# Masked relative queries: from GpSimd, 32 queries at a time into one buffer, to ScalarE, column by column into one of two

## The chip, the cores and the metric

One core of a Trainium2 chip runs the whole program in one launch. The metric is the device time in microseconds (us), a median over runs. Engines are named as in the profile: PE is TensorE (PEld its weight loads), DVE is VectorE, ACT is ScalarE, POOL is GpSimd, SP is SyncE, which here only issues DMAs.

## The reference

A transformer layer over x of shape (16, 1024, 256), with 16 heads of 16:

```python
h = layernorm(x)
q, k, v = heads(h @ Wq.T + bq), heads(h @ Wk.T + bk), heads(h @ Wv.T + bv)
rel = rel_emb[r[None, :] - r[:, None] + 511]        # (1024, 1024, 16)
qk = einsum('bhld,bhrd->bhlr', q, k) / 4 + einsum('bhld,lrd->bhlr', q, rel)
x = x + layernorm(softmax(qk) @ v  -> heads joined @ Wo.T + bo)
x = x + layernorm(base + shared low-rank + routed low-rank, top 2 of 6 experts)
```

Indices of `rel_emb` outside its 1023 rows are clamped. What matters here is the second term of `qk`: for every query its own window of the relative embeddings.

## The kernel before

**Tiles and groups.** The 16 x 1024 rows are 128 tiles (`NT`) of 128 queries. A tile's attention is 16 groups (`NG`), g = 4 jp + k: jp picks 256 of the batch's 1024 keys, k picks 32 of the tile's 128 queries, for all heads. One group's scores are 128 keys x (16 heads x 32 queries), twice (c = 0, 1), in two of PSUM's six score banks; three such pairs (`NBUF`) go round.

**A group on the engines.** PE writes the scores in `scores`: 8 matmuls of `ks` by `qm` (L724) and 12 of the shifted embeddings `tw` by the masked queries `rm` (L730) for each c. DVE takes maxima (L1185), PE transposes them (L738), DVE reduces and spreads them (`spread`: L1194, then `nmm`, L1197), PE adds the negative maxima to the scores (`shift`, L747), and ACT makes `prob` by one Exp (`exp`, L1018). PE multiplies by the values (`pv`, L757) in the next stage's groups k = 1 and 2. PE is one group ahead: its group g ends with the shift of group g - 1, and ACT's group g ends (`before`) with the Exp of group g - 1. So the Exp of a tile's group 14 follows the shift that is PE's last work of the tile, and that of group 15 comes in the next tile's group 0.

**Work of other tiles between.** `wide` and `mixed` on PE, `side` on DVE, the copies in ACT's `tile` and POOL's `tile` carry the projections of the tile 8 later, the output side of the tile before, and the feed-forward part of the one before that. Every engine works through an order written out by hand, and waits on semaphores.

**The masked queries.** `raw` holds the tile's queries in 24 copies of 16 rows (8 groups of 16 partitions x 3 column sets s), which SP loads with 24 DMAs (`load_raw`). `rm` is `raw` times `mask_r`, which is 1 where a partition belongs to a column and 0 elsewhere: for every octet of queries, ten column slots (3 + 4 + 3, `RUNS`). Before the change POOL's `mask(i)` writes the part for the 32 queries i by three multiplications (L592), in one buffer. Part i is last read by group 12 + i, so POOL waits for that group's scores:

```python
if att:                                   # early in the tile
    pool.wait_ge(s_scores, t * NG)
    mask(NI - 1)                          # part 3 of this tile
...
pool.wait_ge(s_raw, ...)                  # late in the tile
pool.wait_ge(s_scores, t * NG + NG - NI + 1)
mask(0)                                   # part 0 of the next tile; then rs2, parts 1 and 2, res
```

PE waits for part k in groups 0 to 3 (L884). SP waits for part 3 before it loads the next tile's queries into `qm` and `raw` (L411). Before the loop POOL writes parts 0 to 2 of the first tile, between the seventh and the eighth split of the prologue's queries and keys.

**The loop.** Tiles 2 to 127 run in a loop of three turns of 42 tiles; `ph` is the tile's number modulo the buffers.

Of the kernel before, what the change touches and what calls it, by code (L numbers as in the profile page):

```python
# [9 lines left out]
H, HD = 16, 16  # L10
# [3 lines left out]
P = 128  # L14
NT = B * L // P
TPB = L // P
JC = L // P
NJP = JC // 2
IW = 32
NI = P // IW  # L20
NG = NJP * NI
# [4 lines left out]
OCT = 8  # L26
RP = 3
RUNS = ((0, 3), (2, 4), (5, 3))
# [16 lines left out]
def sandwich_kernel(nc, x, wqT, bq, wkT, bk, wvT, bv, woT, bo, relT, baseT, base_b,  # L45
# [13 lines left out]
    with ctx:  # L59
        def sb(name, shape, dt=f32):  # L60
            return ctx.enter_context(nc.sbuf_tensor(name, shape, dt))
# [6 lines left out]
        ident16 = sb("ident16", [P, P], f16)  # L68
        pick = sb("pick", [P, H // 2, P], f16)
        mask_h = sb("mask_h", [H, 2, IW], f16)  # L70
        mask_r = sb("mask_r", [P, RN], f16)
        mhalf = sb("mhalf", [P, 1])
        eps = sb("eps", [P, 1])
        one = sb("one", [P, 1])
# [27 lines left out]
        vs = sb("vs", [P, JC, H, 32])  # L102
        raw = sb("raw", [P, RP, H, P], f16)
        qm = sb("qm", [ROWS, 2, H, P], f16)
        rm = sb("rm", [P, NI, IW // OCT, RN * H], f16)
        prob = sb("prob", [P, 2, 2, H, P])
        r1 = sb("r1", [P, H + P], f16)
        nm = sb("nm", [P, 2, P], f16)
# [219 lines left out]
        def _(sp):  # L328
# [63 lines left out]
            def after(sem, value):  # L392


                sp.wait_ge(sem, value)
                sp.sem_inc(s_step, 1)

            def tile(b, it, att, proj, a, bb, new=False, last=False, end=False, wrap=False, first=False):
# [4 lines left out]
                if att:  # L403
                    if not first:

                        after(s_scores, t * NG)
                        load_window(it, NJP - 1)
                        if new:
                            after(s_qkst, n * 64)
                            load_keys(b, NJP - 1)  # L410
                    after(s_mask, t * NI + NI)  # L411
                    if last:
                        load_queries(b + 1, 0)
                        load_raw(b + 1, 0)
                    else:
                        load_queries(b, it + 1)
                        load_raw(b, it + 1)
# [116 lines left out]
        def _(pool):  # L534
# [50 lines left out]
                keep(mask_r[:, c:c + n], ALU.is_ge, lo + half - 1, [[half, n]], -1)  # L585
            pool.drain().then_inc(s_cpool, 1)

            def mask(i):

                for s, ((q, n), c) in enumerate(zip(RUNS, RCOL)):  # L590
                    src = raw[:, s, :, i * IW:(i + 1) * IW].rearrange("p h (m e) -> p m h e", e=OCT)
                    last = g.tensor_tensor(rm[:, i, :, c * H:(c + n) * H].rearrange("p m (h e) -> p m h e", e=n),  # L592
                                           src[:, :, :, q:q + n],
                                           mask_r[:, c:c + n].rearrange("p (a b e) -> p a b e", a=1, b=1)
                                           .to_broadcast((P, IW // OCT, H, n)), ALU.mult)
                last.then_inc(s_mask, 1)

            def rstd(dst, mv, ve):
                g.tensor_tensor(ve[:, :], mv[:, 1:2], eps[:, :], ALU.add)  # L599
                pool.drain()  # L600
# [12 lines left out]
                return x.rearrange("p c i -> p (c i)")  # L613

            def tile(t, n, att, proj, a, b, ph=None):
                if att:
                    pool.wait_ge(s_scores, t * NG)
                    mask(NI - 1)
                if b:
                    pool.wait_ge(s_x1T, t - 1)  # L620
                    split([flat(x1T2[:, k, :, :]) for k in range(2)], flat(x1T[:, :, :]), s_x1T2)
# [54 lines left out]
                if a:  # L676
                    pool.wait_ge(s_xr, t * 16)
                    pool.wait_ge(s_yn, t)
                    g.tensor_tensor(x1[:, :], yn[:, :], xr[:, :], ALU.add).then_inc(s_x1, 1)
                if att:  # L680

                    pool.wait_ge(s_raw, t * (RP * OCT * 16) + 2 * RP * OCT * 16)
                    pool.wait_ge(s_scores, t * NG + NG - NI + 1)
                    mask(0)
                if a:
                    pool.wait_ge(s_mv2, t)
                    rstd(rs2, mv2, ve2).then_inc(s_rs2, 1)
                if att:
                    for i in range(1, NI - 1):
                        pool.wait_ge(s_scores, t * NG + NG - NI + i + 1)  # L690
                        mask(i)
                if b:
                    pool.wait_ge(s_y2n, t - 1)
                    pool.wait_ge(s_out, (t - 1) * 16)
# [4 lines left out]
            pool.wait_ge(s_mv0, 1)  # L699
            rstd(rs0, mv0, ve0).then_inc(s_rs0, 1)  # L700
            for k in range(TPB):
                if k == TPB - 1:
                    pool.wait_ge(s_raw, RP * OCT * 16)
                    for i in range(NI - 1):
                        mask(i)
                pool.wait_ge(s_qkbp, k + 1)
                if k > 1:
                    pool.wait_ge(s_qkst, (k - 1) * 64)
                split([flat(first_h[k % 2][:, :, :]), flat(first_l[k % 2][:, :, :])], flat(qkb[:, :, :]), s_qksp)
# [4 lines left out]
        def _(pe):  # L714
            mm = nc.tensor.matmul

            def scores(g, c, buf, qb):

                jp, i = divmod(g, NI)
                bank = sc[:, 2 * buf + c, :]  # L720
                out3 = bank.rearrange("p (h i) -> p h i", i=IW)
                j = (2 * jp + c) * P
                for h in range(H // 2):
                    last = mm(bank[:, 2 * h * IW:(2 * h + 2) * IW], ks[:, h, j:j + P],  # L724
                              qm[:, qb, 2 * h:2 * h + 2, i * IW:(i + 1) * IW],
                              start=(h == 0), stop=False, skip_group_check=True)
                for m in range(IW // OCT):
                    u = P - 1 - (i * IW + OCT * m) + c * P
                    for s, ((q, n), r) in enumerate(zip(RUNS, RCOL)):
                        last = mm(out3[:, :, OCT * m + q:OCT * m + q + n], tw[:, s, jp, u:u + P],  # L730
                                  rm[:, i, m, r * H:(r + n) * H].rearrange("p (h e) -> p h e", e=n),
                                  start=False, stop=False, skip_group_check=True)
                return last

# [137 lines left out]
            def tile(t, n, att, proj, a, b, ph=None):  # L872
                read = None
                for g in range(NG):
                    jp, k = divmod(g, NI)
                    old = a if g == 0 else att
                    if att:
                        if k == 0:
                            pe.wait_ge(s_tw[jp], t * 16 + 16)
                            pe.wait_ge(s_ks[jp], batch_of(t) * 96 + 96)  # L880
                        if g == 0:
                            pe.wait_ge(s_qm, t * 96 + 96)
                        if jp == 0:
                            pe.wait_ge(s_mask, t * NI + k + 1)  # L884
                        free = t * NG + g - NBUF + 1
                        if not (isinstance(free, int) and free <= 0):
                            pe.wait_ge(s_exp, free)
                        scores(g, 0, buffer(ph, g), ph % 2)
                    if read is not None:
                        pe.wait_ge(*read)  # L890
                    if old:
                        transpose_max(t * NG + g)
                    if att:
                        scores(g, 1, buffer(ph, g), ph % 2).then_inc(s_scores, 1)

                    wide(t, n, g, att, proj, a)
                    read = mixed(t, g, att, a, b)
                    if old:
                        shift(buffer(ph, g - 1), t * NG + g)
# [43 lines left out]
        def _(act):  # L943
# [56 lines left out]
            for k in range(TPB):  # L1000
# [8 lines left out]
                if k == 4:  # L1009
                    first_keys()  # L1010

            def exp(g, buf, count, free):

                jp, i = divmod(g, NI)
# [12 lines left out]
            def tile(t, n, att, proj, a, b, ph=None):  # L1027
                for g in range(NG):
# [54 lines left out]
                        copy(oT[:, :, :].rearrange("p c i -> p (c i)"), p_t).then_inc(s_oT, 1)  # L1083
                    if a if g == 0 else att:
                        before(g, t, ph)

            passes(act, tile)


# [235 lines left out]
```

## Time and profile before

| | |
|---|---|
| median of 3 runs | 5952.92 us (5951.9 to 5957.06) |
| the profiled execution's own time | 5973.55 us |
| its span in the trace | 5971.8 us |
| PE busy | 5815.1 us, 97% |
| DVE, POOL, ACT busy | 4903.6, 3328.2, 3069.3 us (82%, 56%, 51%) |
| POOL's multiplications for `rm` | 1545, 929.9 us |
| granted TensorE clock, mean | 0.994 |

The profiled execution is 0.35% longer than the median; times of single instructions come from it. A span of 5971.8 us over 128 tiles, with some 73 us ahead of the first scores and 50 us behind the last, is about 45.7 us for a tile and 2.86 us for a group.

### The profile page before, as it was taken

The page shows a single profiled execution, that of the slowest core. Times are in us where ns is not written, and L with a number is a line of the kernel's source. Part 1 is how long each engine was busy: PE and PEld are TensorE (multiplying, and loading weights), DVE is VectorE, ACT ScalarE, POOL GpSimd, SP SyncE. Part 2 cuts the span into 40 slices and gives each one's busy share as a digit, 9 for nine tenths or more (in the row PEclk, how much of TensorE's full clock was granted, in tenths as well). Part 3 has the DMA queues.
Part 4 walks back from the last instruction along what each step waited for, and adds up shares of the span by engine and source line. Part 5 has one row for each costly group of instructions (what it writes and reads, how often), then busy time and mean ns, then how long its engine had stood idle before and what let it go on. Part 6 is the DMA issues. An engine that isn't in the chain of part 4 may idle for free.

```text
span 5971.8 us, 378300 instructions
## 1 busy us (share of the span) xinstructions
PE 5815.1 (97%) x161792; PEld 5385.6 (90%) x161792; DVE 4903.6 (82%) x10178; ACT 3069.3 (51%) x5160; POOL 3328.2 (56%) x5182
## 2 busy tenths in 40 slices
PE   6999999999999999999999999999999999999997
PEld 5999999999999999999999899999999999999996
DVE  5888888888888888888888888888888888888886
ACT  3555555555555555555555555555555555555554
POOL 4555555555555555555555555555555555555555
PEclk8999999999999999999999999999999999999998
DMA  5343343443434334343343434334344343433432
GB/s 152 85 102 94 91 116 85 106 102 86 113 91 115 88 87 114 93 110 90 92 110 90 112 94 100 95 90 117 83 107 100 89 110 90 116 87 88 113 95 53
DMA packets 1461087, 589.65 MB, mean 99 GB/s; under 512 B 1127168, under 2 KB 1425136, under 8 KB 1459376
## 3 DMA queue, kind: packets, MB, share of 16 engines
q1 hardware_dynamic: 1454752, 562.48, 37.8%
q8 instruction: 1288, 21.10, 1.6%
q14 instruction: 423, 3.47, 0.2%
q10 hardware_dynamic: 4624, 2.60, 0.2%
HBM read 476.43 MB, written 89.85 MB: 95 GB/s over the span
## 4 chain that ended last, share of the span: by engine, by line
PE 83%; DVE 10%; issue 3%; DVEq 2%; POOL 1%; SPq 0%; POOLq 0%; DMA 0%; ACT 0%
PE sc L730 21%; PE pw L757 15%; PE sc L747 15%; PE sc L724 14%; DVE r L1185 5%; PE pm L778 4%; PE pw L778 4%; PE pm L738 4%; PE pw L764 3%; DVE xn L1099 2%; DVE nmm L1197 1%; DVEq L1196 1%; DVE y2n L1099 1%; PE pm L797 1%; DVEq L1095 1%
## 5 line engine op out<-in xcount | busy, mean ns | idle before, releaser
L1185 DVE TRANSPOSE_TENSOR_REDUCE r<-sc 128x32 f16<-128x1024 f32 x2048 | 2542.9, 1242 | 22.3 <-PE sc L730 19.0
L1018 ACT ACTIVATE prob<-sc 128x1024 f32<-128x1024 f32 x2048 | 2098.8, 1025 | 213.9 <-PE sc L747 176.9
L730 PE MATMUL sc<-rm,tw 128*128 128x48 f16 (+1 forms) x49152 | 2144.6, 194 | 11.6 <-issue 11.4
L730 PEld LDWEIGHTS sc<-rm,tw 128*128 128x128 f16 x49152 | 1754.4, 100 | 13.6 <-issue 13.2
L724 PE MATMUL sc<-qm,ks 96*128 96x64 f16 x32768 | 1635.8, 193 | 23.2 <-POOL rm L592 13.8
L747 PE MATMUL sc<-nmm,pick 128*128 128x64 f16 x32768 | 1297.5, 193 | 40.5 <-DVE nmm L1197 32.1
L724 PEld LDWEIGHTS sc<-qm,ks 96*128 96x128 f16 x32768 | 1298.3, 98 | 35.2 <-issue 21.9
L1194 DVE TENSOR_REDUCE nm<-pm 16x32 f16<-16x256 f32 x2048 | 834.8, 408 | 557.5 <-PE pm L738 540.9
L747 PEld LDWEIGHTS sc<-nmm,pick 128*128 128x128 f16 x32768 | 1128.7, 98 | 179.2 <-DVE nmm L1197 91.3
L757 PE MATMUL pw<-prob,vs 128*32 128x128 f32 x32768 | 1117.9, 276 | 12.5 <-issue 8.1
L757 PEld LDWEIGHTS pw<-prob,vs 128*32 128x32 f32 x32768 | 840.1, 109 | 76.0 <-issue 14.6
L592 POOL TENSOR_TENSOR rm<-raw,mask_r 128x192 f16<-128x192 f16 (+1 forms) x1545 | 888.8, 605 | 20.8 <-DMA raw<-qk_s 18.2
L1197 DVE TENSOR_TENSOR nmm<-nm,mask_h 16x64 f16<-16x64 f16 x2048 | 652.3, 319 | 194.0 <-issue 5.4
L738 PE MATMUL pm<-ident,r 128*128 128x128 f16 x4096 | 571.0, 221 | 1.3 <-issue 0.7
L947 ACT ACTIVATE ot<-pw 128x512 f32<-128x512 f32 x512 | 305.2, 596 | 488.4 <-PE pw L757 488.4
L605 POOL TENSOR_TENSOR oT<-oT,one 128x256 f16<-128x256 f32 x128 | 78.6, 614 | 759.8 <-ACT oT L947 759.8
L947 ACT ACTIVATE nmt<-pm 128x16 f32<-128x16 f32 x512 | 94.3, 184 | 760.0 <-PE pm L797 760.0
L634 POOL TENSOR_TENSOR wp<-parts,wst 128x1088 f32<-128x1088 f32 x128 | 262.7, 2053 | 178.9 <-ACT parts L947 178.9
L764 PE MATMUL pw<-ident,ot 128*128 128x128 f32 x2048 | 324.9, 281 | 0.8 <-ACT ot L947 0.7
L601 POOL TENSOR_TENSOR rs<-ve,mhalf 128x1 f32<-128x1 f32 x513 | 282.2, 550 | 73.7 <-issue 1.3
L605 POOL TENSOR_TENSOR hT<-hT,one 112x128 f16<-112x128 f32 x128 | 51.2, 400 | 488.1 <-ACT hT L947 488.1
L599 POOL TENSOR_TENSOR ve<-mv,eps 128x1 f32<-128x1 f32 x513 | 113.6, 221 | 373.8 <-DVE mv L1096 373.5
(153 smaller groups left out, 5766.2 us busy)
## 6 DMA issues: line engine op xcount, KB each, us to landing
raw<-qk_s SPq DMA_DIRECT2D x3096, 64.0 KB, 2.9
tw<-tw_s SPq DMA_DIRECT2D x512, 288.0 KB, 4.0
v_s<-vpad SPq DMA_DIRECT2D x136, 256.0 KB, 3.4
vs<-v_s SPq DMA_DIRECT2D x64, 512.0 KB, 4.4
qm<-qk_s SPq DMA_DIRECT2D x768, 32.0 KB, 2.1
ks<-qk_s SPq DMA_DIRECT2D x378, 64.0 KB, 3.4
qk_s<-qkh SPq DMA_DIRECT2D x272, 64.0 KB, 2.9
qk_s<-qkl SPq DMA_DIRECT2D x272, 64.0 KB, 2.6
```

What stands on the lines that cost most here:

```text
L592: last = g.tensor_tensor(rm[:, i, :, c * H:(c + n) * H].rearrange("p m (h e) -> p m h e", e=n), src[:, :, :, q:q + n], mask_r[:, c:c + n]. ...
L724: last = mm(bank[:, 2 * h * IW:(2 * h + 2) * IW], ks[:, h, j:j + P], qm[:, qb, 2 * h:2 * h + 2, i * IW:(i + 1) * IW], start=(h == 0), stop ...
L730: last = mm(out3[:, :, OCT * m + q:OCT * m + q + n], tw[:, s, jp, u:u + P], rm[:, i, m, r * H:(r + n) * H].rearrange("p (h e) -> p h e", e=n),
L738: last = mm(p_max[:, c * P:(c + 1) * P], r1[:, c * H:c * H + P], ident16[:, :], start=True, stop=True)
L747: last = mm(pairs[:, :, h, :], pick[:, h, :], nmm[:, :, :], start=False, stop=True, skip_group_check=True)
L757: last = mm(pw[32 * q:32 * q + 32, col * P:(col + 1) * P], vs[:, 2 * jp + c, h, :], prob[:, jp % 2, c, h, :], start=(c == 0), stop=(c == 1))
L764: last = nc.tensor.transpose(pw[:, col * P:(col + 1) * P], ot[:, col, :], ident[:, :])
L778: last = mm(dst, lhs, rhs, start=(m == 0), stop=(m == len(steps) - 1))
L1018: A(prob[:, jp % 2, :, :, i * IW:(i + 1) * IW], sc[:, 2 * buf:2 * buf + 2, :].rearrange("p c (h i) -> p c h i", i=IW), ACT.Exp).then_inc(s ...
L1185: v.tensor_reduce(r1[:, 0:2 * H], sc[:, 2 * buf:2 * buf + 2, :].rearrange("p c (h i) -> p (c h) i", i=IW), axis=AX.X, op=ALU.max, apply_tr ...
L1194: v.tensor_reduce(part, p_max[0:H, :].rearrange("h (q i) -> h i q", i=IW), axis=AX.X, op=ALU.max, negate=True).then_inc(s_nmr, 1)
L1197: v.tensor_tensor(nmm[0:H, :, :], part.rearrange("h (a i) -> h a i", a=1) .to_broadcast((H, 2, IW)), mask_h[:, :, :], ALU.mult).then_inc(s ...
```

## The change

Ten ScalarE operations a tile take the place of POOL's twelve multiplications. Each scales one column slot of `raw` (128 partitions x 256 elements) by one float32 column of `mask_r` (L71, now f32) and writes it to its place in `rm`, which has two halves, one for even and one for odd tiles (L105). In a tile's groups 11 to 15 ACT writes two slots each for the next tile, behind the Exp of `before`; the signal follows the last slot. PE waits for it once a tile, ahead of group 0, in the place of the four waits; SP's wait asks for it by the new count. All slots of tile 0 are written by ACT ahead of its loop. The diff, cut to its core:

```diff
-        mask_r = sb("mask_r", [P, RN], f16)
+        mask_r = sb("mask_r", [P, RN])
-        rm = sb("rm", [P, NI, IW // OCT, RN * H], f16)
+        rm = sb("rm", [P, 2, NI, IW // OCT, RN * H], f16)
@@ SP, tile @@
-                    after(s_mask, t * NI + NI)
+                    after(s_mask, t + 1)
@@ POOL: mask(i) and its calls are gone, in tile and ahead of it @@
-                if att:
-                    pool.wait_ge(s_scores, t * NG)
-                    mask(NI - 1)
...
-                    pool.wait_ge(s_raw, t * (RP * OCT * 16) + 2 * RP * OCT * 16)
-                    pool.wait_ge(s_scores, t * NG + NG - NI + 1)
-                    mask(0)
...
-                    for i in range(1, NI - 1):
-                        pool.wait_ge(s_scores, t * NG + NG - NI + i + 1)
-                        mask(i)
@@ PE, scores and tile @@
-                                  rm[:, i, m, r * H:(r + n) * H]...
+                                  rm[:, qb, i, m, r * H:(r + n) * H]...
                         if g == 0:
                             pe.wait_ge(s_qm, t * 96 + 96)
-                        if jp == 0:
-                            pe.wait_ge(s_mask, t * NI + k + 1)
+                            pe.wait_ge(s_mask, t + 1)
@@ ACT @@
+            def mask(qb, some):
+                for s, q, c, n, e in some:
+                    dst = rm[:, qb, :, :, c * H:(c + n) * H].rearrange("p i m (h e) -> p (i m) h e", e=n)[:, :, :, e]
+                    src = raw[:, s, :, :].rearrange("p h (m e) -> p m h e", e=OCT)[:, :, :, q]
+                    last = A(dst, src, ACT.Identity, scale=mask_r[:, c + e:c + e + 1])
+                return last
...
                     if a if g == 0 else att:
                         before(g, t, ph)
+                    if att and g > 10:
+                        if g == 11:
+                            act.wait_ge(s_raw, t * (RP * OCT * 16) + 2 * RP * OCT * 16)
+                        last = mask((ph + 1) % 2, slots[2 * (g - 11):2 * (g - 10)])
+                        if g == NG - 1:
+                            last.then_inc(s_mask, 1)
+
+            act.wait_ge(s_raw, RP * OCT * 16)
+            mask(0, slots).then_inc(s_mask, 1)
             passes(act, tile)
```

## Rows read from the trace of the kernel before

**Rows 1.** The page: busy time by engine, and the chain that ended last.

```profile
PE 5815.1 (97%) x161792; PEld 5385.6 (90%) x161792; DVE 4903.6 (82%) x10178; ACT 3069.3 (51%) x5160; POOL 3328.2 (56%) x5182
...
PE 83%; DVE 10%; issue 3%; DVEq 2%; POOL 1%; SPq 0%; POOLq 0%; DMA 0%; ACT 0%
```

**Rows 2.** Waits of PE: waited for, us in total, times, longest us.

```profile
PE sc L747 <- DVE nmm L1197: 32.1, 133, 2.2
...
PE sc L724 <- POOL rm L592: 13.8, 3, 10.8
```

**Rows 3.** Timeline, turn of a tile: start us, us, engine, line, work, [idle before].

```profile
3042.85 3.46 POOL L592 TENSOR_TENSOR rm<-raw,mask_r 128x192 f16<-128x192 f16 x6
...
3043.16 0.63 PE L747 MATMUL sc<-nmm,pick 128*128 128x64 f16 x16
...
3043.63 0.40 PE L724 MATMUL sc<-qm,ks 96*128 96x64 f16 x8
3043.83 1.02 ACT L1018 ACTIVATE prob<-sc 128x1024 f32<-128x1024 f32 x1
...
3044.34 0.40 PE L724 MATMUL sc<-qm,ks 96*128 96x64 f16 x8
...
3045.14 0.56 DVE L1197 TENSOR_TENSOR nmm<-nm,mask_h 16x64 f16<-16x64 f16 x1
3045.18 0.38 PE L769 MATMUL pm<-ident,xn 128*128 128x128 f32 x2
...
3045.76 0.64 PE L747 MATMUL sc<-nmm,pick 128*128 128x64 f16 x16 [0.19 <-DVE nmm L1197]
```

**Rows 4.** Timeline of ACT, an Exp with other work queued behind it.

```profile
3049.52 1.03 ACT L1018 ACTIVATE prob<-sc 128x1024 f32<-128x1024 f32 x1 [0.38 <-PE sc L747]
3050.44 0.25 ACT L1056 ACTIVATE wst<-dm 128x64 f32<-128x64 f32 x1
```

**Rows 5.** Groups of instructions by form: busy us, mean ns; idle before, releaser.

```profile
L947 ACT ACTIVATE hT<-pm 112x128 f32<-112x128 f32 x128 | 35.5, 278 | 206.7 <-PE pm L824 206.7
...
L1005 ACT ACTIVATE qkb<-sc,b_qk 128x128 f32<-128x128 f32 x32 | 9.1, 368 | 36.1 <-PE sc L778 25.9 <-POOL qkl L607 10.3
L947 ACT ACT_TABLE_LOAD x1 | 1.3, 1283 | 9.2 <-issue 9.2
...
L947 ACT ACTIVATE w_b<-w_b 112x256 f16<-112x256 f32 x1 | 0.4, 398 | 0.0
```

**Rows 6.** The same view, POOL.

```profile
L592 POOL TENSOR_TENSOR rm<-raw,mask_r 128x256 f16<-128x256 f16 x515 | 314.7, 611 | 0.0
```

**Rows 7.** Line L1197: durations in ns min/median/max, first and last start.

```profile
L1197 DVE TENSOR_TENSOR nmm<-nm,mask_h x2048: 178/180/1056, 75.8 to 5923.9; 16x64 f16<-16x64 f16 x187
```

**Rows 8.** Busy PE in four stretches: PE busy (instructions), granted clock, DMA share, GB/s.

```profile
79.48:82.89 3.41, 1.59 (x49) 1.00 0.57 161
82.89:86.30 3.41, 1.03 (x16) 0.50 0.99 246
5554.46:5561.30 6.84, 5.14 (x144) 1.00 0.80 196
5926.51:5933.33 6.82, 4.40 (x75) 0.75 0.14 41
```

**Rows 9.** Timeline of the prologue's end and of tile 0's group 4.

```profile
69.33 5.07 POOL L592 TENSOR_TENSOR rm<-raw,mask_r 128x192 f16<-128x192 f16 x9 [9.37 <-DMA raw<-qk_s]
71.18 0.59 PE L724 MATMUL sc<-qm,ks 96*128 96x64 f16 x8 [10.84 <-POOL rm L592]
...
87.53 0.58 PE L724 MATMUL sc<-qm,ks 96*128 96x64 f16 x8 [3.25 <-issue]
...
88.77 0.63 PE L724 MATMUL sc<-qm,ks 96*128 96x64 f16 x8
```

**Rows 10.** Waits of SP's queue.

```profile
SPq L479 <- POOL qkl L607: 10.0, 2, 9.8
```

More of the change, by code:

```diff
@@ L586, in _ @@
             pool.drain().then_inc(s_cpool, 1)
[L588 to L596, printed above, removed]
             def rstd(dst, mv, ve):
@@ L679, in tile @@
                     g.tensor_tensor(x1[:, :], yn[:, :], xr[:, :], ALU.add).then_inc(s_x1, 1)
-                if att:
-                    pool.wait_ge(s_raw, t * (RP * OCT * 16) + 2 * RP * OCT * 16)
-                    pool.wait_ge(s_scores, t * NG + NG - NI + 1)
-                    mask(0)
                 if a:
@@ L687, in tile @@
                     rstd(rs2, mv2, ve2).then_inc(s_rs2, 1)
-                if att:
-                    for i in range(1, NI - 1):
-                        pool.wait_ge(s_scores, t * NG + NG - NI + i + 1)
-                        mask(i)
                 if b:
@@ L701, in _ @@
             for k in range(TPB):
[L702 to L705, printed above, removed]
                 pool.wait_ge(s_qkbp, k + 1)
@@ L730, in scores @@
                         last = mm(out3[:, :, OCT * m + q:OCT * m + q + n], tw[:, s, jp, u:u + P],
-                                  rm[:, i, m, r * H:(r + n) * H].rearrange("p (h e) -> p h e", e=n),
+                                  rm[:, qb, i, m, r * H:(r + n) * H].rearrange("p (h e) -> p h e", e=n),
                                   start=False, stop=False, skip_group_check=True)
@@ L1010, in _ @@
                     first_keys()
+            slots = [(s, q + e, c, n, e) for s, ((q, n), c) in enumerate(zip(RUNS, RCOL)) for e in range(n)]
+            def mask(qb, some):
[4 more added lines that the diff above has]
+                return last
             def exp(g, buf, count, free):
```

## The prediction

> **What bounds the kernel now.** I began with the page [rows 1]: PE is busy for 97% of the span and carries 83% of the chain that ended last; DVE has 10% of it, ACT none. So time is won only where PE waits, and lost wherever PE is made to wait. The second view was PE's waits [rows 2]. The largest steady one is the shift waiting for `nmm`, 32.1 us in 133 waits, that is about once a tile and 0.2 us each. PE's wait for POOL's `rm` is 13.8 us, of which 10.8 us is the single wait ahead of the first tile; in the loop POOL's masks are nearly free for PE. The third view was the timeline at the turn of a tile [rows 3], where the reader is to see the order of three things. PE's last shift of the tile, that of group 14, starts at 3043.16. The next tile's first scores start at 3043.63, with no wait. The Exp of group 14 starts only at 3043.83, because it needs that shift. So at the turn ACT is behind PE, and all that stands behind that Exp in ACT's order comes later still.
>
> **What is removed.** POOL loses twelve multiplications a tile. They cost PE almost nothing directly. Indirectly they reach PE through DVE: `nmm` takes 0.56 us at 3045.14 while POOL is masking and 0.18 us otherwise [rows 3, 7], and this is the once-a-tile wait. If `nmm` takes 0.18 us, the shift is held by the transposes ahead of it (3045.18, 0.38 us) instead. The gain is at least the 0.19 us that PE is shown idle, and at most what `nmm` shrinks by, 0.38 us. I take 0.3 us a tile: the transposes' duration overlaps what follows, so the shift can start somewhat before their end.
>
> **What is added on ACT.** Ten Identity operations a tile of 256 elements, SBUF to f16 in SBUF, with a per-partition scale. No row has this. A copy of 256 elements SBUF to f16 takes 398 ns; a column operand adds 368 - 278 = 90 ns (two forms with 128 elements, with and without a bias column) [rows 5]. Together 0.49 us. The bounds: 0.40 us, if the column costs nothing here; above, the strided read and write may cost, for which the nearest row is POOL's multiplication with the same pattern and as many elements, 0.61 us [rows 6], and with the column 0.70 us. I take 0.49 us, since ACT's rows otherwise follow the count of elements. Work queued behind an Exp starts 0.92 us after the Exp's start, 0.11 us before its end [rows 4]; so a second mask starts 0.38 us after the first. Over the tile that is ten times 0.38, 3.8 us more for an engine busy 51%. In groups 11 to 14 it lies under PE's work: a pair adds 0.76 us after an Exp, so ACT is free 1.7 us after the Exp began, in a group of 2.86 us, and the next thing in ACT's order, a copy of what PE makes in the middle or at the end of the group, comes later than that or just then. Without this cover a pair would cost 0.76 us a group.
>
> The masks bring Identity between Exps. The trace shows one table load, at the start, although Identity (`qkb`) ran after Copy and before Exp [rows 5]; so I cost switches at nothing. The Trainium skill, "ScalarE: Activation LUTs", section "What ACT_TABLE_LOAD costs", puts 2.66 us on every switch to another set; by it, were Identity in another set, five groups would pay two switches each, 27 us a tile. The row speaks for one set.
>
> **What is moved: the wait at the turn.** The last pair of masks stands behind the Exp of group 14, and PE may not start the next tile's group 0 before its signal. From [rows 3]: Exp starts 3043.83; first mask 3044.75; second 3045.13; its end 3045.62; the signal and PE's start some 0.05 us later, 3045.67, as PE's start at 3045.76 follows the end of `nmm` at 3045.70 by 0.06. PE would have started at 3043.63. The wait costs 2.04 us. Nothing stands against it: behind the waiting instruction on PE are all of group 0's scores, on which DVE's next maxima and ACT's next Exp depend, so all three stop. What DVE gets is that it has finished group 15's maxima meanwhile; this is why I count the 0.3 us above as given back in full and no more. With the bounds of the mask: 0.20 (3043.63 to the Exp) + 0.92 + 0.29 (0.40 less the overlap of 0.11) + 0.40 + 0.05 = 1.86 us with the cheap one, and 0.20 + 0.92 + 0.59 + 0.70 + 0.05 = 2.46 us with the dear one. Net for a tile 2.04 - 0.3 = 1.74 us; at the bounds 1.86 - 0.38 = 1.48 and 2.46 - 0.19 = 2.27 us. It is paid at the start of tiles 1 to 127: 127 x 1.74 = 221 us (188 to 288).
>
> **The clock.** A PE that pauses can lose its clock. The stretch 79.48 to 82.89, which ends in an idle of about 1.8 us, is followed by one at a granted clock of 0.50, the lower level of 1.2 GHz; the stretch from 5554.46, with 1.7 us of idle in all, stays at 1.00, 2.4 GHz [rows 8]. The new pause would show as 3045.67 - 3043.79 = 1.9 us of idle, right between. Price: 5926.51 to 5933.33 has a mean of 0.75, half of it slow, so a slow stretch can be 3.4 us. At the slow clock the first half of a group took 88.77 - 87.53 = 1.24 us [rows 9], at the full one 3044.34 - 3043.63 = 0.71 us [rows 3]; 3.4 us slow do the work of 1.95 to 2.1 us, so about 1.3 us is lost. I let this happen in a third of the tiles: 42 x 1.3 = 55 us; in none it is 0, in all 165 us.
>
> [...]
>
> **SP and the start.** SP's count changes, and the signal comes 3045.62 instead of the end of part 3's masks, so the loads of `qm` and `raw` move by a few us, with a whole tile to land. They are hidden; without this cover PE would wait at group 0 for `qm`, and ACT at group 11 for `raw`. At the start ACT's ten masks follow the landing of `raw` at 69.33: 9 x 0.38 + 0.49 = 3.9 us, so PE starts at 73.3, not 71.18 [rows 9]: +2.1 us. But POOL's last split of the prologue no longer waits behind nine multiplications; SP's wait of 9.8 us for it [rows 10] goes, the first batch's keys land before group 4, and its wait of 3.25 us and the similar 2.2 us ahead of a shift [rows 2, 9] go, with the slow clock that follows them (about 10 us at 0.50, some 3.9 us). Sum: -7 us.
>
> **The sum.** Against the profiled execution, 5973.55 us: +221 + 55 - 7 = +269 us. That execution is 0.35% above the median of the runs; the same added to the median gives 5952.9 + 269 = 6222 us.
>
> **The rivals.**
> The pause at the turn without any loss of the clock: for it speaks the stretch at 5554.46. 5953 + 221 - 7 = 6167 us.
> The pause and a slow stretch in every tile: for it speaks 79.48, and that the pause comes at the same place each time; against it that 1.9 us is at the edge. 5953 + 221 + 165 - 7 = 6332 us.
> A mask far above 0.70 us because of 2-byte elements at a stride: each 0.1 us more is 127 x 0.2 = 25 us, and from about 1 us a pair would also press on groups 11 to 14: 6400 us and more. No row of ACT has such a pattern.
> No difference: the pause eats waits that PE has anyway. Against it: all of PE's waits in the loop together are far below 221 us [rows 1, 2].
> Faster: ACT is done with the last masks when PE comes to group 0, that is 2.04 us earlier than I work out, before its Exp has even begun. Then the relief of DVE by POOL is all that is left: 5953 - 38 - 7 = 5908 us. The point that decides is the order Exp, masks, signal at the turn; [rows 3] speak against it plainly.
>
> **How the numbers follow.** The pause with some slow stretches 0.50; without any 0.25; with one every tile 0.15; masks far dearer 0.05; no difference 0.03; faster 0.02. The predicted time is that of the first, 6222 us. Its own range with the bounds of the mask is 6160 to 6300. The range for 8 in 10 reaches down past the case without a slow clock and its lower bound, 5953 + 188 - 7 = 6134, and up to the case with one in every tile: 6120 to 6335. Slower by over 0.2% (about what a measurement of this kernel can tell from no change) 0.95, within 0.03, faster 0.02.
>
> **What would show it.** PE's wait at L724 for ACT's `rm`, 127 times with about 1.9 us each, 240 us in all; in the timeline of a turn, Exp, two masks, then PE's first scores. 1290 masks of 0.49 us in ACT's groups, ACT busy about 630 us more, POOL 930 us less. The 32.1 us of waits for `nmm` reduced to a few. A mean granted clock of about 0.98; 0.99 would mean the second case, 0.96 the third. Wrong I would be if that wait were absent or under 1 us, if masks took 0.7 us or more, or if PE waited in groups 11 to 15.

## The result and the profile after

The changed kernel takes 6371.9 us (median of 4 runs, 6367.24 to 6385.57) against 5954.99 us before: a ratio of 1.0704, 95% interval 1.0685 to 1.0722. It is slower, as forecast, but by 417 us and not by 269; 6372 lies above the range of 6120 to 6335 us. The profiled execution took 6385.57 us with a span of 6383.8 us, 412 us more than before.

The page of the changed kernel: busy time by engine, its chain by engine and by line (L698, L704, L721 and L731 are L724, L730, L747 and L757 of before), and its masks:

```profile
PE 5936.7 (93%) x161792; PEld 5568.1 (87%) x161792; DVE 4716.7 (74%) x10178; ACT 3873.6 (61%) x6450; POOL 2470.7 (39%) x3637
...
PE 87%; ACT 9%; issue 2%; DVE 1%; DVEq 1%; SPq 0%; POOL 0%; POOLq 0%; ACTq 0%; DMA 0%
PE sc L704 22%; PE pw L731 16%; PE sc L721 15%; PE sc L698 15%; ACT rm L992 4%; PE pm L752 4%; PE pm L712 4%; PE pw L752 4%; ACT prob L1001 4%; PE pw L738 3%; PE pm L743 1%; PE pm L771 1%; PE pw L743 1%; ACT parts L920 1%; PE pm L798 1%
...
L992 ACT ACTIVATE rm<-raw,mask_r 128x256 f16<-128x256 f16 x1290 | 925.1, 799 | 6.2 <-DMA raw<-qk_s 6.2
```

ACT had 0% of the chain [rows 1]; now it has 9% of it, 4% each in the masks and the Exp. DVE's 10% has shrunk to 1%. A mask takes 799 ns on average. The trace still holds a single table load of 1283 ns, so Identity between the Exps costs no switch. ACT is busy 804 us more than before where 630 were forecast, POOL 857 us less where 930 were. Two of PE's waits in the changed kernel (us in total, times, longest):

```profile
PE sc L698 <- ACT rm L992: 352.5, 128, 13.6
...
PE sc L721 <- DVE nmm L1188: 4.3, 15, 1.1
```

The wait for the masks, less the first tile's 13.6 us, is 338.9 / 127 = 2.67 us of idle a turn. The wait for `nmm`, 32.1 us [rows 2], is nearly gone. One turn in the changed kernel's timeline (start us, us, work):

```profile
2999.26 0.63 PE L721 MATMUL sc<-nmm,pick 128*128 128x64 f16 x16
...
2999.90 0.39 ACT L920 ACTIVATE parts<-pw 128x272 f32<-128x272 f32 x1
3000.17 1.02 ACT L1001 ACTIVATE prob<-sc 128x1024 f32<-128x1024 f32 x1
3000.18 0.37 DVE L1090 TENSOR_SCALAR xn<-x,mv,rs 128x256 f32<-128x256 f32 x1
...
3001.08 1.37 ACT L992 ACTIVATE rm<-raw,mask_r 128x256 f16<-128x256 f16 x2
3002.57 0.60 PE L698 MATMUL sc<-qm,ks 96*128 96x64 f16 x8 [2.68 <-ACT rm L992]
...
3005.80 1.06 PE L721 MATMUL sc<-nmm,pick 128*128 128x64 f16 x16
```

The order is as forecast: PE's last shift, the Exp, two masks, PE's first scores. In [rows 3] the scores follow the start of that shift by 0.47 us, here by 3.31 us: the pause is 2.84 us from start to start, where 2.04 was forecast. Then the shift of 16 matmuls takes 1.06 us instead of 0.64. The same stretch in windows of PE (PE busy, instructions, granted clock, DMA share, GB/s):

```profile
2999.60:3002.57 2.97, 0.29 (x10) 0.90 0.45 140
3002.57:3005.80 3.23, 3.23 (x47) 0.50 0.23 54
3005.80:3009.02 3.22, 3.22 (x60) 0.53 0.36 79
```

After the pause PE works at the lower level of its clock. The mean granted clock is 0.960, where 0.994 was before.

For what follows I measured the turn on the starts of the shifts (L747 before, L721 after): from the shift of group 14 to that of group 15, and from there to that of group 0, as medians over tiles 2 to 127. Before: 2.96 and 3.02 us. After: 6.20 and 3.33 us.

### The profile page after: what moved, and what is told of

Read it like the earlier page. It is cut to its first block, busy times and chain, and to the rows that moved or that the text cites. A ratio compares the mean times of both kernels' runs of the same rounds, so it can differ in the third digit from the quotient of the medians.

```text
span 6383.8 us, 377318 instructions
## 1 busy us (share of the span) xinstructions
PE 5936.7 (93%) x161792; PEld 5568.1 (87%) x161792; DVE 4716.7 (74%) x10178; ACT 3873.6 (61%) x6450; POOL 2470.7 (39%) x3637
## 4 chain that ended last, share of the span: by engine, by line
PE 87%; ACT 9%; issue 2%; DVE 1%; DVEq 1%; SPq 0%; POOL 0%; POOLq 0%; ACTq 0%; DMA 0%
PE sc L704 22%; PE pw L731 16%; PE sc L721 15%; PE sc L698 15%; ACT rm L992 4%; PE pm L752 4%; PE pm L712 4%; PE pw L752 4%; ACT prob L1001 4%; PE pw L738 3%; PE pm L743 1%; PE pm L771 1%; PE pw L743 1%; ACT parts L920 1%; PE pm L798 1%
## 5 line engine op out<-in xcount | busy, mean ns | idle before, releaser
L704 PE MATMUL sc<-rm,tw 128*128 128x48 f16 (+1 forms) x49152 | 2209.1, 197 | 6.3 <-issue 6.1
L698 PE MATMUL sc<-qm,ks 96*128 96x64 f16 x32768 | 1686.1, 195 | 354.2 <-ACT rm L992 352.5
L704 PEld LDWEIGHTS sc<-rm,tw 128*128 128x128 f16 x49152 | 1816.7, 102 | 7.0 <-issue 6.9
L698 PEld LDWEIGHTS sc<-qm,ks 96*128 96x128 f16 x32768 | 1347.8, 100 | 369.2 <-issue 369.2
L721 PE MATMUL sc<-nmm,pick 128*128 128x64 f16 x32768 | 1326.1, 195 | 11.3 <-issue 5.6
L721 PEld LDWEIGHTS sc<-nmm,pick 128*128 128x128 f16 x32768 | 1179.7, 99 | 118.4 <-issue 58.3
L731 PE MATMUL pw<-prob,vs 128*32 128x128 f32 x32768 | 1112.4, 276 | 9.2 <-issue 4.6
L992 ACT ACTIVATE rm<-raw,mask_r 128x256 f16<-128x256 f16 x1290 | 925.1, 799 | 6.2 <-DMA raw<-qk_s 6.2
L731 PEld LDWEIGHTS pw<-prob,vs 128*32 128x32 f32 x32768 | 838.4, 109 | 69.0 <-issue 7.2
L1188 DVE TENSOR_TENSOR nmm<-nm,mask_h 16x64 f16<-16x64 f16 x2048 | 565.7, 276 | 193.9 <-issue 5.4
L712 PE MATMUL pm<-ident,r 128*128 128x128 f16 x4096 | 585.7, 226 | 0.5 <-DVE r L1176 0.4
L595 POOL TENSOR_TENSOR x1T<-x1T,one 128x256 f16<-128x256 f32 x128 | 78.5, 614 | 790.8 <-ACT x1T L920 790.8
```

What stands on the lines that cost most here:

```text
L712: last = mm(p_max[:, c * P:(c + 1) * P], r1[:, c * H:c * H + P], ident16[:, :], start=True, stop=True)
L721: last = mm(pairs[:, :, h, :], pick[:, h, :], nmm[:, :, :], start=False, stop=True, skip_group_check=True)
L731: last = mm(pw[32 * q:32 * q + 32, col * P:(col + 1) * P], vs[:, 2 * jp + c, h, :], prob[:, jp % 2, c, h, :], start=(c == 0), stop=(c == 1))
L992: last = A(dst, src, ACT.Identity, scale=mask_r[:, c + e:c + e + 1])
L1188: v.tensor_tensor(nmm[0:H, :, :], part.rearrange("h (a i) -> h a i", a=1) .to_broadcast((H, 2, IW)), mask_h[:, :, :], ALU.mult).then_inc(s ...
```

## The experiments

**The masks one group earlier (`early`).**

```diff
-                    if att and g > 10:
-                        if g == 11:
+                    if att and 10 <= g < NG - 1:
+                        if g == 10:
...
-                        last = mask((ph + 1) % 2, slots[2 * (g - 11):2 * (g - 10)])
-                        if g == NG - 1:
+                        last = mask((ph + 1) % 2, slots[2 * (g - 10):2 * (g - 9)])
+                        if g == NG - 2:
```

> The masks in groups 10 to 14 instead of 11 to 15, and nothing else. My theory: the added time is the pause of TensorE at the turn of a tile, because the last masks stand behind the Exp of group 14, and the slow clock that follows it. Then the pause is gone, TensorE waits for the masks only ahead of the first tile, the granted clock is 0.99, and what is left is the relief of VectorE and the shorter start: 5900 to 5930 us. The rival: ten masks of 0.8 us each cost time wherever they lie, because ScalarE's copies and Exps come late: then 6050 us or more, with new waits of TensorE for ScalarE in groups 10 to 15.

Measured: 5902.88 us, ratio to before 0.9906 (0.9889 to 0.9922). The same ten masks of 0.8 us on the same engine, and the kernel is faster than before; the rival, masks that cost wherever they lie, falls. PE still waits a little:

```profile
PE sc L698 <- ACT rm L992: 42.4, 117, 14.1
```

**The pause without the masks (`sigexp`).** As `early`, and PE's first group waits for one Exp more:

```diff
-                        free = t * NG + g - NBUF + 1
+                        free = t * NG + g - NBUF + 1 + (g == 0)
```

> Masks in groups 10 to 14, and TensorE's first group of a tile waits for the Exp of group 14 in the place of that of group 13: the pause at the turn without the two masks in it. My theory: the pause shows 1.1 us of idle (0.04 + 1.02 + 0.05), start to start 1.3 us, and is too short to lower the clock: the kernel with the masks one group earlier plus 127 x 1.3 = 165 us, about 6080 us, granted clock 0.99. The rival, that any pause once a tile lowers the clock each time: about 6240 us, clock 0.96.

Measured: 6039.83 us, ratio 1.0143 (1.0126 to 1.016), granted clock 0.993. Its wait in the profile:

```profile
PE sc L698 <- ACT prob L1001: 170.8, 127, 1.4
```

That is 1.34 us of idle a turn, where I expected 1.1. The turn takes 3.77 us against the 2.24 us of a turn without any wait, a pause of 1.53 us: longer than expected, because the two masks of group 14 push the Exp back (see below). The difference to `early` is 137 us all the same, where 165 stood, because `early` itself still lost 0.41 us a turn (2.65 us): 127 x (3.77 - 2.65) = 142 us. The clock stays up, so a pause once a tile does not by itself lower it.

**The pause with its idle time filled (`fill`).**

```diff
-                            pe.wait_ge(s_mask, t + 1)
...
+                        if g == 0:
+                            for _ in range(10):
+                                filler(buffer(ph, g), ph % 2)   # the 8 matmuls of L698, overwritten later
+                            pe.wait_ge(s_mask, t + 1)
```

> The changed kernel, but TensorE runs ten sets of the first 8 score matmuls of the tile (80 matmuls whose results are overwritten, about 2.3 us) ahead of its wait for the masks. The pause remains as long, its idle time is filled. My theory: the slow clock costs 437 us x (1 - 1/1.65) = 170 us of the changed kernel's time, so this one takes 6200 us with a granted clock of 0.99 and 2.8 us from start to start at the turn. The rival: after a pause TensorE has slack anyway, and the slow clock costs little: 6350 us or more.

Measured: 6204.18 us, ratio 1.0413 (1.0396 to 1.043), granted clock 0.993. A turn in its timeline, L711 being the filler and L726 the shift:

```profile
3017.66 0.63 PE L726 MATMUL sc<-nmm,pick 128*128 128x64 f16 x16
3018.16 2.50 PE L711 MATMUL sc<-qm,ks 96*128 96x64 f16 x80
...
3018.59 1.01 ACT L1009 ACTIVATE prob<-sc 128x1024 f32<-128x1024 f32 x1
3019.49 1.39 ACT L1000 ACTIVATE rm<-raw,mask_r 128x256 f16<-128x256 f16 x2
3020.94 0.41 PE L698 MATMUL sc<-qm,ks 96*128 96x64 f16 x8 [0.28 <-ACT rm L1000]
```

The scores still come 3.28 us after the shift, but 8 of them take 0.41 us, not 0.60. The turn is 5.04 us, so the pause costs 5.04 - 2.24 = 2.80 us. The time between this kernel and the changed one, 6371.9 - 6204.2 = 168 us, is the price of the slow clock. Both numbers were expected within 5 us.

**The mask's form by itself (`forms`).** At the end of the changed kernel, with the other engines done, six operations of each form:

```diff
+            for k in range(6):
+                A(strided(k, 0, 3), comb, ACT.Identity, scale=col)      # L1093; L1095 with 4 columns a run
+            for k in range(6):
+                A(dense(k), comb, ACT.Identity, scale=col)              # L1098: dense target
+            for k in range(6):
+                A(strided(k, 0, 3), flat_src, ACT.Identity, scale=col)  # L1101: dense source; L1103 with 4
+            for k in range(6):
+                A(dense(k), flat_src, ACT.Identity, scale=col)          # L1106; L1109 as Copy; L1112 L1093 as Copy
```

> The changed kernel, with 48 more ScalarE operations of 128 x 256 elements at its very end, when the other engines are done: the mask's form with 3 and with 4 columns a run, then one thing changed at a time (a dense target, a dense source, both, no column operand). My estimate of 0.49 us a mask should hold for the dense form with a column, 0.40 us for the dense copy. The measured 0.74 to 0.88 us come, by the first theory, from 2-byte elements written at a stride (a dense target then brings it back to 0.5), by the second from the strided read (a dense source does), by the third from what the other engines do to SBUF meanwhile (then here, alone, even the strided form takes 0.5 us).

ACT's groups by form in its last 60 us (busy us, mean ns):

```profile
L1095 ACT ACTIVATE rm<-raw,mask_r 128x256 f16<-128x256 f16 x6 | 4.0, 856 | 0.0
L1093 ACT ACTIVATE rm<-raw,mask_r 128x256 f16<-128x256 f16 x6 | 3.9, 737 | 0.1
L1098 ACT ACTIVATE rm<-raw,mask_r 128x256 f16<-128x256 f16 x6 | 3.8, 714 | 0.1
L1103 ACT ACTIVATE rm<-raw,mask_r 128x256 f16<-128x256 f16 x6 | 3.6, 808 | 0.0
L1112 ACT ACTIVATE rm<-raw 128x256 f16<-128x256 f16 x6 | 3.3, 634 | 0.1
L1101 ACT ACTIVATE rm<-raw,mask_r 128x256 f16<-128x256 f16 x6 | 3.1, 680 | 0.1
L1106 ACT ACTIVATE rm<-raw,mask_r 128x256 f16<-128x256 f16 x6 | 2.5, 494 | 0.1
L1109 ACT ACTIVATE rm<-raw 128x256 f16<-128x256 f16 x6 | 1.9, 402 | 0.1
```

Dense on both sides the operation takes 494 ns with a column and 402 ns without, as I had put it together from [rows 5]. A strided source (every eighth 2-byte element of each head, read head by head, 128 elements apart) alone brings 714, a strided target alone 680 (steps of 3 elements) or 808 (steps of 4), both together 737 and 856. So it is the stride, of either side, and the two hardly add up. With both sides strided the step of 4 lengthens one operation, but hardly a row of them: six take 3.96 us with steps of 4 and 3.89 us with steps of 3 (with a dense source 3.61 and 3.15). Each of my three readings said too little: no single side brings it back to 0.5, and the other engines have no part in it. The loop's 722 to 897 ns are these same numbers.

**The masks, dense (`plain`).** The changed kernel, source and target dense; the masked queries are taken from and put to other places, so the output isn't the reference's.

```diff
-                    dst = rm[:, qb, :, :, c * H:(c + n) * H].rearrange("p i m (h e) -> p (i m) h e", e=n)[:, :, :, e]
-                    src = raw[:, s, :, :].rearrange("p h (m e) -> p m h e", e=OCT)[:, :, :, q]
+                    flat = rm[:, qb, :, :, :].rearrange("p i m f -> p (i m f)")
+                    dst = flat[:, 2 * P * (c + e):2 * P * (c + e + 1)].rearrange("p (m h) -> p m h", h=H)
+                    src = raw[:, s, 0:2, :].rearrange("p a t -> p (a t)").rearrange("p (m h) -> p m h", h=H)
```

> The changed kernel with masks whose source and target are both dense, 256 elements as before (they leave the masked queries wrong, the scores too; counts and waits are the same). In the form alone this took 494 ns, my 0.49 us. My theory: two masks take 0.38 + 0.49 = 0.87 us instead of 1.38, and the pair in group 14 no longer pushes the copy and the Exp behind it by 0.24 us, so the pause is 2.1 us, 0.75 us less than 2.84: 127 x 0.75 = 95 us less with the clock as slow as before, 6277 us; up to 165 us less again if the clock stays up. It shows what my sum gives once the mask costs what I took, and so how much of the error is not the mask's.

Measured: 6244.67 us, ratio 1.0476 (1.0458 to 1.0493), granted clock 0.971. The mask takes 501 ns in the loop, and PE waits:

```profile
PE sc L698 <- ACT rm L993: 265.9, 128, 13.6
```

252.3 / 127 = 1.99 us a turn. With the mask at the price I took, the kernel is 23 us from my 6222 us. But not all of that is merit, as the next section shows.

**One mask fewer behind the Exp (`late1`).** 3, 2, 2, 2 and 1 masks in groups 11 to 15:

```diff
+                        first = (0, 3, 5, 7, 9, 10)
-                        last = mask((ph + 1) % 2, slots[2 * (g - 11):2 * (g - 10)])
+                        last = mask((ph + 1) % 2, slots[first[g - 11]:first[g - 10]])
```

> The changed kernel with 3, 2, 2, 2 and 1 masks in groups 11 to 15: one mask of 0.64 us less behind the Exp of group 14. The pause goes from 2.84 to 2.20 us (idle from 2.68 to 2.04), 127 x 0.64 = 81 us less. What it tells is the clock: an idle of 2.04 us is about the pause that I had predicted. With a slow stretch at every turn as before: 6291 us and a clock of 0.96. With one at a third of the turns, as I took it: 6180 us and 0.98. With none: 6125 us and 0.99.

Measured: 6255.17 us, ratio 1.0492 (1.0474 to 1.0509), granted clock 0.977; idle (250.9 - 14.6) / 126 = 1.88 us a turn, a little under the 2.04 that I expected. The clock lies between the cases: neither all nor none.

**The masks ahead of the Exp (`swap`).** Group 15's pair before the Exp of group 14, the rest as in the changed kernel:

```diff
+                    if att and g == NG - 1:
+                        mask((ph + 1) % 2, slots[8:10]).then_inc(s_mask, 1)
                     if a if g == 0 else att:
                         before(g, t, ph)
-                    if att and g > 10:
+                    if att and 10 < g < NG - 1:
```

> The changed kernel with one thing in another order: in group 15 the two masks stand ahead of the Exp of group 14 instead of behind it. They can start 0.1 us before the end of the copy in front of them, which ends some 0.6 us after the last shift of the tile begins, and take 1.38 us, so the signal comes about 1.9 us after that shift's start, where the next scores would come at 0.47. My theory, that the place behind the Exp made the pause: it falls from 2.84 to between 1.4 and 1.7 us and is now too short to lower the clock, so the time is 5873 + 127 x 1.5 = 6065 us (6050 to 6090), clock 0.99. The rival, that the late Exp now stops TensorE in the next group instead: over 6150 us.

Measured: 6174.67 us, ratio 1.0359 (1.0342 to 1.0376), granted clock 0.976. The place behind the Exp is confirmed as a part of the pause: 197 us are gone by the order alone, and the idle falls to (239.2 - 15.5) / 127 = 1.76 us. But the expectation of 6050 to 6090 us missed by 85 us, in two terms. The slow clock, which I had at nothing, came at 65 turns of the profiled execution (65 x 1.33 = 86 us): I had taken such a pause for short enough, and it is not. And the pause itself was longer than the 1.4 to 1.7 us expected: as medians the scores come 2.41 us after the shift, a pause of 2.41 - 0.47 = 1.94 us. I had let the copy ahead of the masks end 0.6 us after the shift, as in the kernel before; behind the two masks of group 14 it ends at 1.02 us. The rival's new stop in the next group does not show: where the clock stayed up, the group after the turn takes 2.92 us, as in `best`, so the late Exp is covered.

**The relief alone (`tiny`).** The kernel before, GpSimd's masks in the loop cut to one head and the first octet; waits, signals and order stay.

```diff
+            def touch(i):
+                    last = g.tensor_tensor(rm[:, i, 0, c * H:c * H + n], raw[:, s, 0, i * IW + q:i * IW + q + n],
+                                           mask_r[:, c:c + n], ALU.mult)
-                    mask(NI - 1)
+                    touch(NI - 1)
```

> The kernel before, with GpSimd's masks in the loop cut down to one head and the first octet of each part (all waits, signals and the order remain; the masked queries of later tiles are wrong). It measures the relief alone. At the turn VectorE's normalization took 0.88 us and its spread 0.56 us beside the masks, and 0.37 and 0.18 us in the changed kernel. My theory: all of the relief is this, by GpSimd's work on SBUF: the turn goes from 2.96 to 2.24 us and the group after it from 3.02 to 2.92, 127 x 0.82 = 104 us less than before, 5850 us. The rival, that the relief in the changed kernel comes from the pause, in which VectorE catches up: then this kernel gains 40 us at most.

Measured: 5892.99 us, ratio 0.989 (0.9873 to 0.9906). The turn falls from 2.96 to 2.28 us and the group after it from 3.02 to 2.93, nearly as expected, 0.77 us a tile. In the whole kernel 67 us are gained between the medians, and 84 between the spans of the two profiled executions (5971.8 and 5887.7); 127 x 0.77 would be 98. The rest lies in tiles off the median and is not settled. The rival, 40 us at most, falls: the relief is there without any pause.

**The start alone (`start`).** The kernel before, with GpSimd's first masks behind its last split of the prologue.

```diff
-                if k == TPB - 1:
-                    pool.wait_ge(s_raw, RP * OCT * 16)
-                    for i in range(NI - 1):
-                        mask(i)
...
+            pool.wait_ge(s_raw, RP * OCT * 16)
+            for i in range(NI - 1):
+                mask(i)
```

> The kernel before, with GpSimd's nine first multiplications moved behind its last split of the prologue, nothing else. My theory: TensorE begins the scores at the same time, 71 us, but its stop of 3.25 us before group 4 of the first tile and the 2.2 us ahead of a shift are gone, and part of the slow clock with them: 7 us less than before. The rival: the keys then arrive earlier but GpSimd's masks come later by as much, and nothing is won.

Measured: 5947.4 against 5957.49 us, ratio 0.9984 (0.9975 to 0.9993): 10 us, where 7 was expected. The first scores come at 71.23 us, those of group 4 at 81.20 instead of 87.53 [rows 9]. The gain holds.

**The better version (`best`).** Two, two, three, two and one masks in groups 10 to 14:

```diff
+                    if att and 10 <= g < NG - 1:
...
+                        first = (0, 2, 4, 7, 9, 10)
+                        last = mask((ph + 1) % 2, slots[first[g - 10]:first[g - 9]])
+                        if g == NG - 2:
+                            last.then_inc(s_mask, 1)
```

> The masks in groups 10 to 14, but 2, 2, 3, 2 and 1 of them instead of 2 each. With two in group 14 TensorE still waited 0.24 us at 116 turns, and its turn took 2.65 us from shift to shift, where without a wait 2.24 us are left (0.47 + 1.77). My theory, that the waits are set by what stands ahead of the last mask in ScalarE's order: the turn takes 2.24 us, 127 x 0.41 = 52 us less than the kernel one group earlier, 5850 us. The rival: three masks in group 12 make the copy that follows them late and give as much back there: 5900 us.

Measured: 5872.58 us, ratio to before 0.9854 (0.9837 to 0.987). PE waits for the masks once, ahead of tile 0, and the turn is 2.25 us:

```profile
PE sc L698 <- ACT rm L992: 15.6, 1, 15.6
PE sc L698 <- issue: 12.6, 13, 3.0
```

The turn is where I expected it. Of the 52 us to `early` only 30 arrive; three masks in group 12 cost nothing that a median shows (2.91 and 2.87 us around it, as before). The tile has gone from 44.82 to 44.42 us as a sum of medians, but only from 45.16 to 44.93 as a mean: more tiles are disturbed, by scattered waits like that of the second line, whose cause the profile doesn't name. It beats both kernels: 1.5% faster than before, 7.8% less time than the changed one (5872.6 / 6371.9).

## Why the prediction was wrong, step by step

**Direction and place: right.** The wait at the turn exists 127 times, in the order foretold, and `early` removes the slowness by moving the same work one group. The sum was wrong in three terms: the pause (+102 us) and the clock (+113 us) were too small in it, and a relief too small by 66 us took part of that back.

| term | predicted, us | measured, us | from |
|---|---|---|---|
| pause at the turn | 127 x 2.04 = 259 | 127 x 2.84 = 361 | changed kernel's timeline; `fill` 2.80 |
| slow clock | 55 | 168 | changed kernel less `fill` |
| relief of DVE | 127 x 0.3 = -38 | 127 x 0.82 = -104 | medians of the turn; 67 to 84 in the whole of `tiny` |
| start | -7 | -5 to -7 | tile 0's shift of group 14 at 117.1 us, before at 121.6; `start` -10, longer first masks +3 |
| sum | 269 | 418 to 420 | measured 417 |

The relief is (2.96 - 2.24) + (3.02 - 2.92) = 0.82 us a tile, with the two groups as `best` has them. With the 67 to 84 us of `tiny` in its place the sum is 438 to 457, so the agreement within 3 us is partly luck. Whole kernels show where: from before to `best` 82 us are gained (relief and start), from `best` to `fill` 332 are lost (the pause), from `fill` to the changed kernel 168 (the clock). Against these the medians overstate the pause by 29 us and the gains by 27 to 29. Which waits outside the median turn make up these some 30 us, 0.5% of the time, is not settled.

**The mask's price: the step that failed first.** "I take 0.49 us, since ACT's rows otherwise follow the count of elements." It was 0.74 to 0.88 us, above even my upper bound of 0.70, and "if masks took 0.7 us or more" was one of the signs that I had named for being wrong. `forms` shows that the count holds only for dense operands. The dense price itself was right to about 5 ns. Of the 0.80 us that the pause was longer than forecast, 0.48 us are the two masks behind the Exp, 0.07 us the signal (scores 0.12 us after the last mask's end, not 0.05), and 0.24 us a step that was missing: with two masks of this price in group 14, the copy behind them starts late and pushes the Exp. As medians over tiles 2 to 127, copy and Exp start 0.18 and 0.68 us after the shift of group 14 in the kernel before, and 0.64 and 0.92 us after it in the changed one. The sentence that in groups 11 to 14 all "comes later than that or just then" was true for masks of 0.49 us: in `plain` it is 0.20 and 0.67 us, no push. In `late1`, where the masks of group 14 are another pair and start earlier, it is 0.44 and 0.72 us: the copy is late, the Exp hardly, and so the idle there was 1.88 us and not the 2.04 expected.

**The clock: wrong share, right price.** "I let this happen in a third of the tiles." Counted in the trace's record of the clock, it happened at 91 of 127 turns, and at 35 of them twice as long: 126 slow stretches (a double one counted as two), 430 us together. The mean clock says the same: twice (1 - clock) x span is 2 x 0.040 x 6383.8 = 511 us, of which `best`, with no pause, has 2 x 0.006 x 5870.8 = 70 us, nearly all at its start and end; 441 us are left. The price, 168 / 126 = 1.33 us a stretch, is what I took from [rows 3, 9]. The pauses in the order of their idle time:

| kernel | idle a turn, us | mean clock | turns of 127 with a slow stretch | stretches |
|---|---|---|---|---|
| `sigexp` | 1.34 | 0.993 | 0 | 0 |
| `swap` | 1.76 | 0.976 | 65 | 65 |
| `late1` | 1.88 | 0.977 | 60 | 62 |
| `plain` | 1.99 | 0.971 | 85 | 85 |
| changed | 2.67 | 0.960 | 91 | 126 |

At the 1.9 us that I had forecast, half of the turns would have been right and a third was low; at 2.67 us there is one stretch a turn on average. That is the price of the rival "a slow stretch in every tile", to which I gave 0.15. The length of the idle alone does not decide: in the changed kernel its median is 2.68 us both at the 91 turns with a slow stretch and at the 36 without. What does is open. The counts are of one execution each and vary: the four of `swap` have mean clocks of 0.976 to 0.982, the 65 turns belong to the lowest. My evidence for the edge was also read too short: the stop at the end of the stretch from 79.48 shows as 1.8 us inside it but goes on to 83.25, 2.18 us in all [rows 2].

**The range.** By its own terms the first case with the bounds of the mask gives 6189 to 6289 us, not 6160 to 6300. And the upper end of 6335 took every slow stretch with a mask of 0.49 us; with the dear mask as well it is 5953 + 288 + 165 - 7 = 6399 us, above the measured time. The two bounds were never put together.

**The relief: read from an untypical turn.** "The gain is ... at most what `nmm` shrinks by, 0.38 us." [rows 3] show a turn of 2.60 us; only 14 of 126 turns take less than 2.7 us, the median is 2.96 us. It follows a gap of 0.62 us of PE that ended 3.25 us earlier, at 3039.91; that DVE had caught up in it is my reading. Its normalization was stretched too, but less, which I overlooked:

```profile
3044.08 0.64 DVE L1099 TENSOR_SCALAR xn<-x,mv,rs 128x256 f32<-128x256 f32 x1
```

Most turns of the kernel before look like this one:

```profile
3133.33 0.64 PE L747 MATMUL sc<-nmm,pick 128*128 128x64 f16 x16
...
3133.38 3.45 POOL L592 TENSOR_TENSOR rm<-raw,mask_r 128x192 f16<-128x192 f16 x6
...
3133.94 0.40 PE L724 MATMUL sc<-qm,ks 96*128 96x64 f16 x8
...
3134.38 0.88 DVE L1099 TENSOR_SCALAR xn<-x,mv,rs 128x256 f32<-128x256 f32 x1
...
3135.17 0.40 DVE L1194 TENSOR_REDUCE nm<-pm 16x32 f16<-16x256 f32 x1
...
3135.67 0.56 DVE L1197 TENSOR_TENSOR nmm<-nm,mask_h 16x64 f16<-16x64 f16 x1
...
3136.28 0.64 PE L747 MATMUL sc<-nmm,pick 128*128 128x64 f16 x16 [0.21 <-DVE nmm L1197]
```

Beside POOL's masks two of DVE's operations are stretched, not one: the normalization takes 0.88 us (0.37 in the changed kernel) and `nmm` 0.56 (0.18). PE follows both, and the turn takes 2.95 us. The idle of 0.21 us in the last row shows only the end of it. As medians after the shift of group 14, the first scores start at 0.59 us in the kernel before and at 0.47 in `best`, the second transposes at 2.31 and 2.03, the next shift at 2.96 and 2.25: a part is lost at each step. `tiny` shows that 0.77 us a tile of this belongs to POOL's masks alone; there `nmm` takes 0.18 us and the normalization still 0.56. That DVE and POOL hinder each other in SBUF is how I read the durations; the runs show that they go together, not by what means.

**What would have been the result with the mask at its price.** `plain` came out at 6244.67 us, inside the range, since its clock (85 stretches of 1.33, 113 us) and its relief were both larger than I had them, by 58 and 66 us. A close number by luck, from two errors.

## What to carry to other kernels

Work handed to an engine with idle time is paid for where its signal stands in that engine's order: with the same ten operations the kernel is 7% slower than before when two of them stand behind the Exp of group 14, and 1.5% faster when they lie one group earlier, spread by what each group can cover. Price an operation by a row with its strides, not only its count; where none exists, widen the bound well beyond the dense price. Read a recurring place in several tiles and take the median, because a single turn may follow a gap that hides the wait.

## What the runs showed of the hardware

ScalarE operations of 128 x 256 elements of 2 bytes take 494 ns dense, 680 to 808 ns with one side at a stride, 737 and 856 ns with both; the step of 4 elements in the target makes one operation some 120 ns longer than the step of 3, but a row of six with both sides strided only 0.07 us (`forms`, one execution). A pause of TensorE with 1.34 us of idle once in 46 us left the clock at 0.993, idles of 1.76 to 1.99 us were followed by a slow stretch at half to two thirds of the turns, one of 2.67 us at 91 of 127, often by a double one. The Trainium skill, "TensorE: Matmul & The Clock Gate", section "HAM oscillation — how this bites in real kernels", describes a lost clock at every single pass of a loop whose waits last about 3 to 5 us. Here shorter idles did it, of 1.76 us at 65 of 127 turns and of 2.67 us at 91, and the measurement decides. Filling the idle with matmuls whose results are thrown away gave 168 of 6372 us back.
